# An attention and mixture-of-experts kernel: 71 pauses between indirect transfers taken out, and the engines' lists of work rewritten

## What is computed

```
xn  = layernorm(x)
s   = where(causal, xn @ qk @ xn.T / sqrt(128), -inf)
att = softmax(s) @ xn @ ov
eid = argmax(xn @ centroids.T)                    # one of 8 experts for each token
alpha = sigmoid(sum(xn * centroids[eid]))
xln = layernorm(xn) * ln_g[eid] + ln_b[eid]
ffn = relu(xln @ w1[eid] + b1[eid]) @ w2[eid] + b2[eid]     # 128 -> 512 -> 128
out = x + att + (xn + alpha * ffn)
```

## Time and profile before

| | |
|---|---|
| median of 3 runs | 223.2 us (222.75 to 223.32) |
| the profiled execution, first to last instruction | 223.1 us |
| PE busy | 206.3 us (92%), 2428 instructions |
| DVE busy | 175.5 us (79%), 448 instructions |
| ACT busy | 155.2 us (70%), 346 instructions |
| POOL busy | 154.3 us (69%), 230 instructions |
| mean granted TensorE clock, share of full | 0.985 |

### The profile page before, as it was taken

One profiled execution on the slowest core, in us unless ns is written; L12 is line 12 of the kernel. 1 busy time (PEld: TensorE's weight loads), 2 busy tenths in 40 slices (PEclk: granted clock), 3 DMA queues, 4 the chain that ended last, 5 costly groups with the idle time before them and its releaser, 6 DMA issues.

```text
span 223.1 us, 6878 instructions
## 1 busy us (share of the span) xinstructions
PE 206.3 (92%) x2428; PEld 159.9 (72%) x2428; DVE 175.5 (79%) x448; ACT 155.2 (70%) x346; POOL 154.3 (69%) x230
## 2 busy tenths in 40 slices
PE   7699776999979999999999999799999999999993
PEld 5544323768856875777766889799999996787773
DVE  6588999899899999999999875556448575535995
ACT  2639989784578899777748755646665658868781
POOL 6173759994259999989999338998999899960000
PEclk9859999999999999999999999999999999999999
DMA  6992003397001111111111696536683111116964
GB/s 167 314 289 64 6 0 94 116 355 232 5 12 39 36 39 39 44 43 40 36 40 36 128 198 160 125 92 141 131 150 92 50 40 37 38 35 172 256 193 141
DMA packets 37601, 23.55 MB, mean 106 GB/s; under 512 B 12472, under 2 KB 34144, under 8 KB 37568
## 3 DMA queue, kind: packets, MB, share of 16 engines
q1 hardware_dynamic: 34960, 18.28, 32.3%
q0 software_dynamic: 2272, 4.69, 6.3%
q10 hardware_dynamic: 336, 0.14, 0.3%
HBM read 11.17 MB, written 9.38 MB: 92 GB/s over the span
## 4 chain that ended last, share of the span: by engine, by line
PE 77%; DVE 11%; ACT 4%; issue 4%; DMA 2%; SPq 1%; DVEq 0%; ACTq 0%
PE psum L1343 6%; PE psum L1300 6%; PE psum L1301 6%; PE psum L1302 6%; PE psum L1351 6%; PE psum L1344 6%; PE psum L1277 5%; PE psum L1460 4%; PE psum L1461 4%; PE psum L1462 4%; PE psum L1434 4%; PE psum L1436 4%; PE psum L1435 4%; PE psum L1260 3%; PE psum L1334 2%
## 5 line engine op out<-in xcount | busy, mean ns | idle before, releaser
L910 DVE TENSOR_TENSOR p_lo<-p_sb,p_hi 128x512 f16<-128x512 f32 (+1 forms) x68 | 42.0, 638 | 12.2 <-ACT p_sb L1050 12.0
L1044 ACT ACTIVATE p_hi<-psum 128x512 f16<-128x512 f32 (+1 forms) x68 | 37.1, 547 | 19.4 <-PE psum L1351 14.2
L1050 ACT ACTIVATE p_sb<-psum 128x512 f32<-128x512 f32 (+1 forms) x80 | 42.5, 539 | 6.8 <-PE psum L1334 6.7
L693 POOL DMA_INDIRECT sorted_y<-xn x39 | 38.1, 977 | 11.6 <-ACT xn L1174 5.5
L1018 DVE SCALAR_TENSOR_TENSOR h_lo<-psum,h_hi 128x512 f16<-128x512 f32 x39 | 26.8, 690 | 21.5 <-ACT h_hi L1166 18.7
L671 POOL MEMSET v_full<- 1x600 f32 x71 | 41.7, 588 | 0.0
L684 POOL DMA_INDIRECT sorted_x<-xr,pos x32 | 33.5, 1047 | 11.9 <-issue 11.4
L1166 ACT ACTIVATE h_hi<-psum 128x512 f16<-128x512 f32 x39 | 23.3, 597 | 21.0 <-PE psum L1436 19.2
L1343 PE MATMUL psum<-v_hi,p_hi 128*128 128x129 f16 x236 | 32.7, 220 | 1.2 <-DVE x_sb L927 1.2
L896 DVE TENSOR_REDUCE row_max<-psum 128x1 f32<-128x512 f32 x48 | 32.3, 682 | 1.6 <-PE psum L1277 1.1
L1344 PE MATMUL psum<-v_lo,p_hi 128*128 128x128 f16 x236 | 32.6, 219 | 0.0
(11 more groups left out here) (189 smaller groups left out, 528.4 us busy)
## 6 DMA issues: line engine op xcount, KB each, us to landing
w_raw<-in_L_ffn_w SPq DMA_DIRECT2D x16, 256.0 KB, 4.2
sorted_x<-zero SPq DMA_DIRECT2D x3, 780.0 KB, 6.4
xn<-sorted_x SPq DMA_DIRECT2D x8, 260.0 KB, 3.9
x_sb<-in_L_attn_input_data SPq DMA_DIRECT2D x8, 256.0 KB, 5.6
xn<-sorted_y SPq DMA_DIRECT2D x8, 256.0 KB, 4.9
out<-x_sb SPq DMA_DIRECT2D x6, 256.0 KB, 3.3
sorted_y<-xn POOLq DMA_INDIRECT x39
sorted_x<-xr,pos POOLq DMA_INDIRECT x32
```

What stands on the lines that cost most here:

```text
L693: pool.indirect_dma_start(out=sorted_y[:, :], out_offset=bass.IndirectOffsetOnAxis(ap=tokens, axis=0), in_=xs[:, t % SLOTS, 0:P], in_offse ...
L910: v.tensor_tensor(p_lo[:, u, off:GW], p_sb[:, u, off:GW], p_hi[:, u, off:GW], ALU.subtract).then_inc(s_plo, 1)
L1044: a.activation(p_hi[:, u, off:GW], bank[SCORE[n % R]][:, off:GW], ACT.Exp, scale=SCALE).then_inc(s_exph, 1)
L1050: a.activation(p_sb[:, u, off:GW], bank[SCORE[n % R]][:, off:GW], ACT.Exp, scale=SCALE).then_inc(s_exp, 1)
```

## The change

The pauses go: the constant `IDLE`, the slice `idle`, the semaphore `s_idle`, `pass_time()` and its two calls. `APART` stays at 3. `ORDER` has the same 1120 entries in another order. The diff of the code:

```
-    IDLE = 600
...
-        idle = flat(v_full[:])[0:1, 0:IDLE]
...
-        s_idle = sem("s_idle")
...
-            pauses = [0]
-
-            def pass_time():
-
-                if pauses[0]:
-                    pool.wait_ge(s_idle, pauses[0])
-                else:
-                    pool.wait_ge(s_pv, N_FULL)
-                    pool.wait_ge(s_vhi, FULL)
-                    pool.wait_ge(s_vlop, FULL)
-                pool.memset(idle, 0.0).then_inc(s_idle, 1)
-                pauses[0] += 1
...
             def send_rows(i):
...
                 transfers.append((s_sent[i % SENT], 16 * (i // SENT + 1)))
-                pass_time()
...
             def store_rows(t):
...
                 transfers.append((s_yst[t % DUMPS], 16 * (t // DUMPS + 1)))
-                pass_time()
```

More of the change, by code:

```diff
@@ L68 @@
 ORDER = entries("""
[L69 to L123, removed]
@@ L129 @@
-X.79 P.75 PB.75 P.76 PB.76 P.77 EH.77 EX.77 EH.78 EX.78 PB.77 P.78 P.79 PB.78 EH.79 EX.79 QT.1.3.0 QT.1.3.1 SO.38 PB.79
+VAR.0.1 LE.0.1 LE.1.2 C0a C1a AE.0 WU C0 C1 C2 T.0 W1.0 W1.1 T.1 VAR.1.2 RN.0.1 ROW.0.1 C2v ROW.1.2 BIAS Tl.0 C1v C2a
+BIASa Ta.0 AE.1 VAR.2.3 Z.0 MISC RN.1.2 RN.2.3 BASE.0 BASE.1 BASE.2 RN.3.4 RN.4.6 RN.6.8 BASE.3 BASE.4 BASE.5 BASE.6 S.0
+S.1 S.2 COL0 S.3 BASE.7 S.4 S.5 S.6 W2l.0 W2l.1 W2l.2 Vl.0 VAR.3.4 Tl.1 VAR.4.6 Ql.0 Ql.1 MR.0.0.3.0 V.0 W1b.0 W1b.1 Q.0
+Q.1 W1.2 M.0.0.3.0 Z.1 Z.2 MR.0.0.2.0 MR.0.0.1.0 MR.0.0.0.0 RM.0.0 VAR.6.8 Tl.2 Z.3 M.0.0.2.0 M.0.0.1.0 M.0.0.0.0 V.1
@@ new lines @@
+T.2 W1.3 M.0.1.3.1 M.0.1.1.0 M.0.1.2.1 W1b.2 W1b.3 M.0.1.1.1 M.0.1.0.1 MR.0.1.3.1 MR.0.1.1.0 MR.0.1.2.1 MR.0.1.1.1
+MR.0.1.0.1 ROW.4.6 Q.2 MR.0.1.3.0 Ql.2 ROW.6.8 SH.0.0 M.0.1.3.0 W1.4 M.0.1.0.0 M.0.1.2.0 W1.5 M.0.2.3.1 M.0.2.3.2
+M.0.2.1.0 X.0 M.0.2.0.2 X.1 MR.0.1.0.0 MR.0.1.2.0 R2 RM.0.1 MR.0.2.3.1 MR.0.2.3.2 MR.0.2.0.2 MR.0.2.1.0 MR.0.2.2.0 AE.2
+W1h.0 W1h.1 Ta.1 Vf.0 W1l.0 LE.2.3 LE.3.4 Qa.0 W1l.1 AE.3 Qa.1 LE.4.6 XA.2 AE.4 AE.5 Ta.2 Vf.1 W1h.2 W1h.3 Va.0 LE.6.8
+W1l.2 W1l.3 Va.1 Qa.2 AE.6 SHa.0.0 XA.3 XA.5 W1h.4 W1h.5 R2a XA.7 SHa.0.1 EX.0 EX.1 EX.2 W2.0 W2.1 Ta.3 Ta.4 Ta.5 Ta.6
@@ new lines @@
+Ta.7 EX.3 Qa.3 EX.4 EX.5 EX.6 EX.7 EX.8 SHa.0.2 Sh.0 Sh.1 EX.9 EX.10 W2.2 W2.3 EX.11 W2.4 Va.2 EH.12 EH.13 EX.12 EX.13
+EH.14 EX.14 Sh.2 EH.15 EH.16 EX.15 EX.16 EH.17 W2.5 EX.17 Sh.3 Sh.4 EH.18 AE.7 EH.19 EH.20 EX.18 EX.19 EX.20 SGa Va.3
+Va.4 SHa.0.3 EH.21 EH.22 EH.23 EX.21 EX.22 Va.5 EX.23 Va.6 Qa.4 M.0.2.2.0 X.2 SH.0.1 M.0.2.0.0 M.0.2.1.2 R2n MR.0.2.0.0
+MR.0.2.1.2 M.0.2.1.1 M.0.2.0.1 M.0.2.3.0 X.3 X.4 M.0.2.2.1 T.3 T.4 X.5 T.5 P.0 T.6 T.7 Q.3 MR.0.2.1.1 MR.0.2.0.1
+MR.0.2.3.0 W1l.4 MR.0.2.2.1 W1l.5 Tl.3 Tl.4 Tl.5 Tl.6 Tl.7 Ql.3 MR.0.2.2.2 QT.0.0.0 QT.0.0.1 RM.0.2 MR.0.3.1.0
@@ new lines @@
+MR.0.3.2.0 P.1 P.2 P.3 M.0.2.2.2 M.0.3.1.0 X.6 M.0.3.2.0 AFF.0 X.7 X.8 AFFr.0.1 AFFr.0.2 AFFr.0.3 AFF.1 AFFr.1.1
+AFFr.1.2 AFFr.1.3 M.0.3.3.1 SH.0.2 P.4 P.5 X.9 X.10 P.6 M.0.3.3.2 P.7 M.0.3.1.1 CNT CH.0 CH.1 MR.0.3.3.1 MR.0.3.3.2
+MR.0.3.1.1 PL MR.0.3.3.3 QT.0.1.0 QT.0.1.1 Vl.2 MR.0.3.2.3 MR.0.3.0.2 XL.12 XL.13 XL.14 MR.0.3.1.3 Sl.0 M.0.3.3.3 X.11
+V.2 P.8 P.9 X.12 P.10 P.11 X.13 X.14 M.0.3.2.3 M.0.3.0.2 P.12 P.13 M.0.3.1.3 X.15 X.16 PB.12 P.14 PB.13 X.17 M.0.3.2.1
+M.0.3.0.3 PB.14 P.15 M.0.3.2.2 X.18 X.19 P.16 P.17 PB.15 M.0.3.1.2 M.0.3.0.1 M.0.3.3.0 PB.16 PB.17 X.20 M.0.3.0.0 P.18
@@ new lines @@
+RM.0.3 XL.18 XL.19 XL.20 Vl.3 SIG Vl.4 BLK XL.21 XL.22 XL.23 Vl.5 Vl.6 Ql.4 MR.1.0.1.0 MR.1.0.3.0 QT.0.2.0 QT.0.2.1
+XL.24 XL.25 XL.26 Ql.5 Ql.6 Sl.3 Sl.4 Vl.7 XL.27 XL.28 MR.1.0.0.0 MR.1.0.2.0 RM.1.0 MR.1.1.0.0 MR.1.1.2.0 XL.29 XL.30
+MR.1.1.1.1 MR.1.1.0.1 MR.1.1.1.0 Vl.1 W2l.3 W2l.4 SC.0 SC.1 SC.2 S.7 W2l.5 SC.3 SC.4 SC.5 SC.6 SC.7 SC.8 SC.9 SC.10
+SC.11 SC.12 SC.13 SC.14 SC.15 SC.16 SC.17 SC.18 SC.19 SC.20 SC.21 SC.22 SC.23 SC.24 SC.25 SC.26 SC.27 SC.28 SC.29 SC.30
+SC.31 W2l.6 W2l.7 Sl.5 XL.31 MR.1.1.3.1 MR.1.1.2.1 MR.1.1.3.0 XL.32 XL.33 RM.1.1 MR.1.2.2.1 XL.34 MR.1.2.3.1 MR.1.2.1.0
@@ new lines @@
+RE.22 RE.23 RE.24 YS.10 YS.11 RE.25 RE.26 RE.27 YS.12 RE.28 RE.29 RE.30 YS.13 YS.14 RE.31 RE.32 RE.33 RE.34 RE.35 YS.15
+YS.16 RE.36 RE.37 RE.38 HI.0 PB.50 PB.51 M.1.3.0.1 HI.1 HI.2 M.1.3.1.0 OUT.0 XL.47 XL.48 RM.1.2 XL.49 MR.1.3.3.0
+MR.1.3.0.2 XL.50 XL.51 QT.1.1.0 QT.1.1.1 LO.0 LO.1 MR.1.3.0.1 LO.2 LO.3 LO.4 LO.5 LO.6 LO.7 MR.1.3.1.2 LO.8 LO.9 LO.10
+LO.11 MR.1.3.1.0 LO.12 LO.13 LO.14 LO.15 LO.16 LO.17 LO.18 LO.19 LO.20 LO.21 LO.22 LO.23 LO.24 LO.25 LO.26 LO.27
+MR.1.3.0.0 MR.1.3.1.3 MR.1.3.0.3 LO.28 LO.29 LO.30 LO.31 LO.32 LO.33 MR.1.3.3.1 MR.1.3.2.2 LO.34 MR.1.3.3.2 LO.35 LO.36
@@ new lines @@
+MR.1.3.3.3 LO.37 LO.38 MR.1.3.2.1 MR.1.3.2.3 MR.1.3.2.0 XL.52 HI.3 OUT.1 HI.4 OUT.2 OUT.3 HI.5 HI.6 OUT.4 HI.7 OUT.5
+OUT.6 HI.8 OUT.7 HI.9 HI.10 SH.1.2 OUT.8 HI.11 OUT.9 HI.12 OUT.10 OUT.11 M.1.3.0.0 HI.13 HI.14 OUT.12 HI.15 OUT.13 HI.16
+OUT.14 OUT.15 HI.17 HI.18 OUT.16 HI.19 OUT.17 HI.20 OUT.18 OUT.19 HI.21 HI.22 OUT.20 HI.23 M.1.3.0.3 OUT.21 HI.24 OUT.22
+OUT.23 HI.25 M.1.3.1.3 HI.26 OUT.24 HI.27 OUT.25 OUT.26 HI.28 HI.29 OUT.27 HI.30 OUT.28 OUT.29 HI.31 M.1.3.2.2 HI.32
+M.1.3.3.1 OUT.30 HI.33 OUT.31 OUT.32 M.1.3.3.2 HI.34 HI.35 M.1.3.3.3 OUT.33 HI.36 OUT.34 OUT.35 HI.37 HI.38 M.1.3.2.3
@@ new lines @@
+M.1.3.2.0 OUT.36 M.1.3.2.1 X.52 X.53 X.54 OUT.37 P.52 P.53 X.55 PB.52 M.1.3.1.1 X.56 X.57 PB.53 OUT.38 P.54 PB.54 SH.1.3
+X.58 P.55 P.56 P.57 PB.55 X.59 PB.56 PB.57 X.60 X.61 P.58 P.59 PB.58 X.62 X.63 P.60 P.61 PB.59 PB.60 X.64 PB.61 P.62
+P.63 X.65 PB.62 PB.63 X.66 XL.53 MR.1.3.1.1 RM.1.3 XL.54 XL.55 XL.56 XL.57 XL.58 XL.59 XL.60 XL.61 Y.6 XL.62 XL.63
+QT.1.2.0 QT.1.2.1 XL.64 XL.65 XL.66 Y.0 Y.7 XL.67 XL.68 Y.3 Y.2 XL.69 XL.70 Y.1 Y.5 XL.71 XL.72 XL.73 Y.4 XL.74 XL.75
+XL.76 XL.77 XL.78 XL.79 EH.52 EH.53 EX.52 EX.53 EH.54 YS.17 YS.18 EX.54 EH.55 EH.56 EX.55 EX.56 YS.19 EH.57 EX.57
@@ new lines @@
+SHa.1.3 EH.58 EX.58 EH.59 EH.60 EX.59 EX.60 EH.61 EX.61 EH.62 EH.63 EX.62 EX.63 EH.64 EX.64 EH.65 EH.66 EX.65 EX.66
+EH.67 EH.68 EX.67 EX.68 EH.69 EH.70 EX.69 EX.70 EH.71 EH.72 EX.71 EX.72 EH.73 EH.74 EX.73 EX.74 EH.75 EX.75 EH.76 X.67
+P.64 P.65 PB.64 X.68 PB.65 P.66 P.67 X.69 PB.66 X.70 PB.67 P.68 P.69 PB.68 X.71 X.72 PB.69 P.70 P.71 X.73 PB.70 SO.0
+SO.1 SO.2 SO.3 SO.4 SO.5 SO.6 SO.7 SO.8 SO.9 SO.10 SO.11 SO.12 SO.13 SO.14 SO.15 SO.16 SO.17 SO.18 SO.19 SO.20 SO.21
+SO.22 SO.23 SO.24 SO.25 SO.26 SO.27 SO.28 SO.29 SO.30 SO.31 SO.32 SO.33 SO.34 SO.35 SO.36 SO.37 X.74 PB.71 P.72 PB.72
@@ L130 @@
+P.73 X.75 X.76 P.74 PB.73 P.75 X.77 PB.74 X.78 X.79 PB.75 P.76 PB.76 P.77 EX.76 EH.77 EX.77 EH.78 EH.79 EX.78 PB.77 P.78
+P.79 PB.78 EX.79 QT.1.3.0 QT.1.3.1 SO.38 PB.79
 """)
```

20 lines of the change are left out of this document (15 added, 5 removed).

## The result

The changed kernel takes 226.8 us (median of 4 runs, 226.3 to 228.9), the kernel before 223.3 on the same chip: ratio 1.0162, 95% interval 1.0126 to 1.0198. It is 3.5 us slower, where 220.5 was forecast. So the span of 223.1 shown of before goes with a time of about 224.8, and its median time with a span of about 221.5.

The account below looks back on a forecast made before the run. The prediction took the kernel as fed too slowly at its start and bound by TensorE alone from 70 us on. It summed 223.1 - 1.9 (start) - 1.1 (YS.3) + 0.4 (Y loads) = 220.5 us, range 218.3 to 224.6.

Parts of the forecast that it names:

- The pace of the transfers: GpSimd's 32 `send_rows` transfers: 1.22 us each without the pause, 1.05 of transfer plus a gap of 0.17.
- rival (a): Transfers at the experts' start need the pause anyway; at 1.72 us each 236.5 us, deciding from 1.34 on; chance 0.13.
- The bound of 1.72: Upper bound in us for one `send_rows` transfer, if it needs the time that the pause filled.
- The sum: Whole kernel: 223.1 less 1.9 (start) less 1.1 (YS.3) plus 0.4 (Y loads) gives 220.5 us.
- Start, 1.9 us: Reordered first list entries bring VAR.2.3 from 14.97 to 13.05; TensorE passes the 1.9 us on, bounds 0 and 3.8.
- OUT.10, 1.1 us: Inside the experts: moving YS.3 before RE.9 removes TensorE's wait for ScalarE's `xn`; 1.1 us off, bounds 0 and 1.8.
- The sums at the end, 0.4 us: Y.6 moves forward on VectorE, so its loads may come a little late: 0.4 us added, bounds 0 and 2.0.
- The pauses by themselves, 0 us: Removing GpSimd's pauses between transfers directly buys nothing, as the rows landed just in time for TensorE.
- The port, 0 us: S.7 and W2l.5, moved to about 83 to 86 us, cost VectorE nothing; 2.4 us if both meet a `p_lo`.
- rival (c): S.7 and W2l.5 clash with `p_lo` while TensorE has no slack: 222.9 us, 224.5 with late Y loads; chance 0.07.
- Pauses cost VectorE nothing: From 70 to 121 us `p_lo` beside transfers and pauses took its usual 680 ns, so removing pauses returns nothing.

Follow-up runs that it names:

- old_list_w2l_late: Kernel before (old list) without pauses, with GpSimd's W2l.5 and W2l.6 held until XL.46 is done: ratio 1.0012 to the kernel before.
- start_only: Kernel before, pauses kept, with only the first entries of the new list on ScalarE, VectorE and GpSimd: 221.7 us, ratio 0.9921 to the kernel before.
- new_list_pauses: Changed kernel with the pauses (`pass_time()`) put back: 246.5 us, ratio 1.0987 to the kernel before.
- old_list_no_pause: Kernel before (old list) with the pauses taken out and nothing else: 225.9 us, ratio 1.0094 to the kernel before.
- release_early: Changed kernel with SGa (ScalarE) and SIG (VectorE) moved forward to release the transfers earlier: 222.9 us, ratio 0.9943 to the kernel before.
- best1: Changed kernel with SGa and SIG early, several Sl, Sh.7, S.7 and W2l entries moved, three W2l held: 223.2 us, ratio 0.9985 to the kernel before.

## Why the prediction was wrong

**What failed.** The pace of the transfers, the term on which rival (a) turns: 1.22 was put, 1.34 was named as the point from which it decides, and it is 1.38. Of the 5.1 us by which 32 of them were longer, some 1.5 are the three longer gaps, which go with APART 4. The rest is 0.30 us in place of 0.17 between two transfers; that stays with APART 4, so it is no wait for a landing, and what it is stays open. The 0.17 was read behind a clearing; it was not the gap between two transfers. An estimate from the rows: at 1.22 the transfers would have ended at 116.1 (74.87 + 39.0 + 2.2), and the first `hidden`, which came 4.5 us behind their end, at 120.7, 1.2 us behind TensorE's arrival instead of 6.4. (The bound of 1.72 was wrong too, without effect: the old list shows 63.67 to 120.51, 1.78 each.)

**And what it was set against.** The sum let the end of the transfers move with the gain of the start, and so priced them at nothing. TensorE came to the first `hidden` at 119.5, where the sum had it near 124. The transfers began at 74.87, 2.5 us earlier than the sum had it (79.3 less 1.9), and ended at 121.33, where the sum gives 118.7. The wait between the two is a difference of two large terms, each with a list of its own, and the sum took both gains as one.

**The sum as it came out,** against the old list in old_list_w2l_late (spans, as their times stand at 1.0162 and 1.0012): first `hidden` 125.87 against 124.37, 1.5 later. From there to the end 99.0 against 97.0, 2.0 more, of which 1.9 is the half clock. Together 3.5, the measured loss.

**Start, 1.9 us.** Right: 1.8 us by start_only, and in the way that was forecast: with BASE.0 behind it ROW.1.2 takes 1.10 us instead of 2.28. In the changed kernel C2 begins at 7.30 (7.9 forecast) and VAR.2.3 at 11.29 (13.05); 0.8 us of this is the execution's earlier first product (5.59 against 6.39). TensorE came 4.7 us earlier to the experts (119.5 against 124.2 in old_list_w2l_late), of which 1.2 is the earlier first product (5.59 against 6.75). That leaves 1.7 us over the 1.8, and where they arise stays open. EX.15 and EX.18 are 6.0 us apart instead of 9.3, where SIG, Vl, BLK, Ql and Sl no longer stand among the XL, but EX.18 and EX.40 are 35.9 apart instead of 31.7, and EX.40 and EX.46 6.7 instead of 8.9. The prediction had counted these entries only as GpSimd's delay. All of the gain went into the wait.

**The clock** stood in no term. In the kernel before it falls as well behind TensorE's wait of 1.98 us: the page has the granted clock in tenths for 40 slices of 5.6 us, and the third, 11.2 to 16.7 us, is at half. The prediction did not ask what the clock does behind the wait of rival (a).

```profile
PEclk9859999999999999999999999999999999999999
```

**OUT.10, 1.1 us.** Wrong, in the reading: the row puts the wait down to ScalarE's `xn`, which happened to end with it, while TensorE was loading the experts' numbers. The gap is 1.14 us in the old list and 1.23 in the new, and moves with LOAD_REST.

**The sums at the end, 0.4 us.** Right in size. Y.6 waits 0.38 us for its loads in the changed kernel (VectorE):

```profile
200.82 0.69 DVE L919 TENSOR_TENSOR x_sb<-x_sb,xn 128x512 f32<-128x512 f32 x1 [0.38 <-DMA xn<-sorted_y]
```

TensorE waits once for a `p_lo` from 185 us on, 0.3 us. But the loads moved by 3.8 us (from 201.50 to 197.74) and Y.6 by 5.1, where some 8 to 10 were put for both the earlier trace rows; that their difference came out as 0.4 is in part luck. Where `store_rows` is slow the same wait is 7.3 us (new_list_pauses).

**The pauses by themselves, 0 us.** Right only with the order of the neighbours kept: taken out alone they cost 2.1 us by W2l, and nothing once W2l is held (1.0012).

**The port, 0 us, rival (c).** Right for the changed kernel: S.7 and W2l.5 met no `p_lo` that counts. But the same clash costs three other kernels here 1.6 to 2.1 us each (old_list_no_pause, release_early, best1). "Pauses cost VectorE nothing" holds: 681 ns for the median `p_lo` from 70 to 121 us, 680 before.

**The scale.** The sum was made on a span and set beside times, as if nothing lay outside it; as a time its 220.5 would have been 222.2, still faster. The execution that it was read from was itself some 1.6 us over the median (224.8 against 223.2), and the two slips nearly cancel; that is luck.

## What to carry to other kernels

Where a transfer is just in time, work out both sides together: when the consumer will arrive, and when the last transfer will land, each by its own list. A gap read behind one kind of instruction is not the gap behind another; bound it from both sides and see whether the bound changes the sign. A filler that does nothing may still decide which neighbours meet on a shared port, so take it out alone before the list is written anew for it.

## What the runs showed of the hardware

A transfer's own instruction was longer than 1.0 us only beside a VectorE instruction with two SBUF inputs (`p_lo` or `xr`). In the 32 transfers of `send_rows` in the thirteen traces, leaving out the first of each, 137 of the 322 that overlapped one were longer (up to 1.50 us), and none of the 81 that did not. Landing is 2.3 to 2.7 us behind the start for most, but 4.0 for the one at 96.66 in the changed kernel, and with APART 3 the third transfer behind waited for it (the gap of 0.83 us). Each of the three longer gaps there ends 0.8 us behind the landing of the third transfer before it.

TensorE stood 1.1 to 1.2 us at the 19 numbers that it loads behind HI.12, and a profile can put that down to another engine whose last work happened to end then.
